# A mixed sequence model on one core: the gate behind the last scores, written out step by step

## The reference, cut to what matters

```python
x = x + _L1_attn_ref(_layernorm(x), Wqa, Wqb, Wkva, Wkvb, Wout, bout)   # latent attention, 16 heads, causal
h = _layernorm(x)
gate_logits = einsum('bsd,de->bse', h, Wg) + bg
topk_w, topk_i = top_k(gate_logits, 2); topk_w = softmax(topk_w)
w = sum(one_hot(topk_i, 8) * topk_w[..., None], axis=-2)
g = gelu(einsum('bsd,edf->bsef', h, W1) + b1)          # 8 experts, 128 -> 512
out = einsum('bsef,efd,bse->bsd', g, W2, w) + einsum('bse,ed->bsd', w, b2)
x = x + out
```

## Time and profile before

| | |
|---|---|
| median of 3 runs | 2117.47 us (2115.41 to 2117.84) |
| profiled execution | 2117.03 us, its span in the profile 2113.9 us |
| instructions | 64856 |
| PE busy | 2001.8 us (95%) |
| DVE busy | 1531.6 us (72%) |
| ACT busy | 1692.8 us (80%) |
| POOL busy | 1454.2 us (69%) |
| mean granted TensorE clock | 0.980 of full |

### The profile page before, as it was taken

The page is one execution under the profiler, slowest core; times in us unless marked ns, Lnnn a source line. Parts: engine busy times, 40 slices in busy tenths (PEclk is TensorE's granted clock), DMA queues, the critical chain, the costliest instruction groups (busy, mean ns, idle before and its releaser), DMA issues. The chain is left out here.

```text
span 2113.9 us, 64856 instructions
## 1 busy us (share of the span) xinstructions
PE 2001.8 (95%) x21603; PEld 1401.2 (66%) x21611; DVE 1531.6 (72%) x3516; ACT 1692.8 (80%) x4279; POOL 1454.2 (69%) x1662
## 2 busy tenths in 40 slices
PE   6899999999999999999999999999999998999596
PEld 3566666666666666666667666666666665666496
DVE  7777777777777777777777777777777764788654
ACT  4688888888888888898989898989898986666355
POOL 5777777777777777777777878787877762244333
PEclk8999999999999999999999999999999999999888
DMA  4222232322232222322222322223544242000023
GB/s 112 52 60 64 48 95 58 73 47 63 65 83 64 61 50 60 84 69 63 56 55 74 81 66 56 54 59 84 120 98 104 49 108 85 2 11 14 18 57 107
DMA packets 191397, 138.95 MB, mean 66 GB/s; under 512 B 47759, under 2 KB 183637, under 8 KB 191173
## 3 DMA queue, kind: packets, MB, share of 16 engines
q1 hardware_dynamic: 189028, 133.09, 26.6%
q0 software_dynamic: 2272, 4.72, 0.7%
HBM read 28.36 MB, written 14.96 MB: 20 GB/s over the span
## 5 line engine op out<-in xcount | busy, mean ns | idle before, releaser
L977 ACT ACTIVATE pr<-bank,mx 128x64 f32<-128x64 f32 x1536 | 336.9, 348 | 0.3 <-DVE mx L1080 0.2
L1162 POOL TENSOR_TENSOR qr<-t 128x512 f32<-128x512 f32 x192 | 245.8, 1280 | 121.0 <-DVE t L1060 120.9
L1059 DVE TENSOR_TENSOR t<-bank,rot_t 128x512 f32<-128x512 f32 x384 | 263.0, 685 | 88.5 <-PE bank L814 86.2
L1150 POOL TENSOR_TENSOR qr<-qr,rn 128x512 f32<-128x512 f32 x192 | 200.8, 1046 | 173.0 <-DVE rn L1031 173.0
L1060 DVE TENSOR_TENSOR t<-bank,rot_t 128x512 f32<-128x512 f32 x384 | 261.5, 681 | 0.0
L1168 POOL TENSOR_TENSOR sqh<-sq 128x512 f32<-128x512 f32 x192 | 246.0, 1281 | 0.0
L1165 POOL TENSOR_TENSOR kr<-t 128x512 f32<-128x512 f32 x192 | 245.3, 1278 | 0.0
L939 ACT ACTIVATE sq<-bank 128x512 f32<-128x512 f32 x192 | 114.4, 596 | 158.2 <-DVE t L1060 158.1
L985 ACT ACTIVATE kBD<-bank 64x512 f32<-64x512 f32 x384 | 228.9, 596 | 3.9 <-PE bank L532 1.6
L814 PE MATMUL bank<-wqkv,xs 128*128 128x512 f32 x384 | 208.3, 625 | 9.1 <-ACT sq L939 2.3
L865 PE MATMUL bank<-kBD,qT 128*32 128x128 f32 x6144 | 207.5, 276 | 0.4 <-ACT bank L919 0.3
(11 more groups left out here) (267 smaller groups left out, 4389.2 us busy)
## 6 DMA issues: line engine op xcount, KB each, us to landing
vBD<-vS SPq DMA_DIRECT2D x1152, 64.0 KB, 2.0
vBD<-vS SPq DMA_DIRECT2D x576, 32.0 KB, 1.9
wqkv<-in_L_ffn_Wqkv_dram SPq DMA_DIRECT2D x12, 768.0 KB, 6.6
rows<-const SPq DMA_DIRECT2D x4, 2244.0 KB, 11.5
wo<-in_L_ffn_Wo_dram SPq DMA_DIRECT2D x12, 256.0 KB, 2.9
t<-rows SPq DMA_DIRECT2D x39, 66.0 KB, 1.9
vBD<-in_L_ffn_W_dram SPq DMA_DIRECT2D x1, 2048.0 KB, 8.6
vBD<-in_L_ffn_W_dram SPq DMA_DIRECT2D x8, 256.0 KB, 7.1
```

Source lines behind the costliest of these rows:

```text
L977: ins = act.activation(pr[:, slot % 2, hd, :], bank[5][:, hd * 64:(hd + 1) * 64], ACT.Exp, bias=mx[:, slot % 2, hd:hd + 1])
L1059: dve.tensor_tensor(t1[:, m], src, tab[:, 0, :].unsqueeze(1).broadcast_to([P, HH, DH]), ALU.mult)
L1150: pool.tensor_tensor(x, x, rn[:, slot, half * HH:(half + 1) * HH].unsqueeze(2).broadcast_to([P, HH, DH]), ALU.mult).then_inc(norm.sem, 1)
L1162: pool.tensor_tensor(qr[:, slot].rearrange("p (h d) -> p h d", d=DH), t1[:, 0], t2[:, 0], ALU.add).then_inc(q_add.sem, 1)
```

## The change

- `pairs()` ends at s = 8; what the loop did at s = 9, 10 and 11 is written out for each engine in an order of its own. LAST = NB - 2 = 6.
- DVE: choose_place and choose_rows of sequence 5 come before normalise_values(7); the residual add of sequence 7 is followed at once by its moments; choose_member(6) comes before the normalise of 7, choose_rows(6) before choose_bias(7). The step numbers of `d_ch` follow the new order.
- A third home for rows, `xg[2]`, in the tile `wo`, with a third set of slots, is used for sequence 7, whose normalise and twin copies so no longer wait for sent rows.
- PE: the transposes of `wA` for groups 0 to 2 (sequences 0 to 5) are issued behind choose_logits(6), ahead of the output projection of sequence 7; bias groups 0 and 1 are issued ahead of the counts of sequence 6 and of sequence 7; only group 3 of the transposes and bias groups 2 and 3 follow the last count. Banks are W_BANK and B_BANK. ACT keeps the turned weights in the same order.
- The number of instructions for each kind of work stays as it was.

```diff
-        slot_u = [late[:, 216 + 4 * k:220 + 4 * k].bitcast(U32) for k in range(2)]
+        slot_u = [late[:, o:o + 4].bitcast(U32) for o in (216, 220, 232)]
         count = late[:, 224:224 + NE]
         xg = [x[:, :, :, :].rearrange("p m h d -> p (m h d)")[:, 0:NSLOT * NT * ROWN].rearrange("p (m t c) -> p m t c", m=NSLOT, t=NT)
-              for x in (t1, t2)]
+              for x in (t1, t2)] + [wo[:, :, :].rearrange("p c k -> p (c k)")[:, 0:NSLOT * NT * ROWN].rearrange("p (m t c) -> p m t c", m=NSLOT, t=NT)]
...
-        LN_STEPS, LOGIT, ROWS, ROW_SET, ROWS_END, DIFF, MEMBER, PLACE, GATE_STEPS = 3, 1, 1, 9, 12, 14, 18, 20, 20
+        LN_STEPS, ROW_SET, ROWS_END, DIFF, MEMBER, PLACE, GATE_STEPS = 3, 8, 11, 14, 18, 20, 20
+        LAST = NB - 2
+        def logit_step(g):
+            return 1 if g < LAST else ROWS_END + 1
+        def row_step(g, n):
+            return n + 1 if g + 1 < LAST else n
         TABLE = 12
+        W_BANK, B_BANK = (4, 5, 6, 6), (7, 4, 5, 0)
...
-            for s in range(1, NB + C_LAG):
+            for s in range(1, NB + 1):
...
-            link(dve, ins, g, ROWS_END + 1)
+            link(dve, ins, g, ROWS_END + 2)
...
-            pool.wait_ge(d_ch.sem, d_ch.after(g + 1, ROW_SET))
+            pool.wait_ge(d_ch.sem, d_ch.after(g + 1, row_step(g, ROW_SET)))
...
+            last = NQ * NB - 1
+            pe.wait_ge(c_ptd.sem, c_ptd.after(2 * last + 1))
+            choose_counts(pe, LAST - 1)
+            pe.wait_ge(c_pta.sem, c_pta.after(2 * last + 1))
+            choose_turn(pe, LAST, LAST % 2)
+            values(NB - 1, 2, 0)
+            values(NB - 1, 2, 1)
+            choose_logits(pe, LAST)
+            for g in range(NGR - 1):
+                choose_back(pe, g)
+            pe.wait_ge(c_nrm.sem, c_nrm.after(NB - 1))
+            for t in range(NT):
+                mm = pe.matmul(low[:, t * P:(t + 1) * P], con[:, t * P:(t + 1) * P], wout[:, :], start=True, stop=True)
+            mm.then_inc(c_y.sem, 1)
+            choose_shift(pe, 0)
+            choose_counts(pe, LAST)
+            choose_turn(pe, NB - 1, 2)
+            choose_logits(pe, NB - 1)
+            choose_shift(pe, 1)
+            choose_counts(pe, NB - 1)
...
+            choose_place(dve, LAST - 1)
+            choose_rows(dve, LAST - 1, (LAST - 1) % 2)
+            normalise_values(NB - 1)
+            choose_bias(dve, LAST)
+            dve.wait_ge(c_y.sem, c_y.after(NB - 1))
+            x = acc[:, seq_cols(NB - 1)]
+            dve.tensor_tensor(x, bank[0][:, 0:SEQ], x, ALU.add).then_inc(c_res.sem, 1)
+            gate_moments(dve, NB - 1)
+            choose_member(dve, LAST)
+            gate_normalise(dve, NB - 1, 2, False)
+            choose_place(dve, LAST)
+            choose_rows(dve, LAST, LAST % 2)
+            choose_bias(dve, NB - 1)
+            choose_member(dve, NB - 1)
+            choose_place(dve, NB - 1)
+            choose_rows(dve, NB - 1, 2)
...
+            send_rows(pool, LAST - 1, (LAST - 1) % 2)
+            gate_rsqrt(pool, NB - 1)
+            twin_rows(pool, NB - 1, 2, False)
+            send_rows(pool, LAST, LAST % 2)
+            send_rows(pool, NB - 1, 2)
+        def choose_back(pe, g):
+            k = g * TG // NT + TG // NT
+            pe.wait_ge(d_ch.sem, d_ch.after(k, row_step(k - 1, ROWS_END)))
+            if g == NGR - 1:
+                pe.wait_ge(d_wTev.sem, d_wTev.after(g - 1))
+            for t in range(TG):
+                mm = pe.transpose(bank[W_BANK[g]][0:NE, t * P:(t + 1) * P], wA[:, g * TG + t, :], ident)
+            mm.then_inc(d_wT.sem, 1)
+        def choose_shift(pe, g):
+            pe.wait_ge(d_wTev.sem, d_wTev.after(g))
+            if g == NGR - 1:
+                pe.wait_ge(c_res.sem, c_res.after(NB - 1))
+            for t in range(TG):
+                o = (g * TG + t) * P
+                mm = pe.matmul(bank[B_BANK[g]][:, t * P:(t + 1) * P], dwT[:, o:o + P], b2e[:, :], start=True, stop=True)
+            mm.then_inc(d_b2.sem, 1)
         def gate_pe(pe):
-            pe.wait_ge(d_ch.sem, d_ch.after(NB, ROWS_END))
+            pe.wait_ge(d_ch.sem, d_ch.after(NB, row_step(NB - 1, ROWS_END)))
             pe.matmul(bank[3][:, 0:NE * NT], cst("ones"), run, start=True, stop=True).then_inc(d_count.sem, 1)
-            for g in range(NGR):
-                for t in range(TG):
-                    mm = pe.transpose(bank[4 + g][0:NE, t * P:(t + 1) * P], wA[:, g * TG + t, :], ident)
-                mm.then_inc(d_wT.sem, 1)
-            for g in range(NGR):
-                pe.wait_ge(d_wTev.sem, d_wTev.after(g))
-                if g == 3:
-                    pe.wait_ge(d_tab.sem, 1)
-                for t in range(TG):
-                    o = (g * TG + t) * P
-                    mm = pe.matmul(bank[g][:, t * P:(t + 1) * P], dwT[:, o:o + P], b2e[:, :], start=True, stop=True)
-                mm.then_inc(d_b2.sem, 1)
+            choose_back(pe, NGR - 1)
+            for g in range(2, NGR):
+                choose_shift(pe, g)
+        def keep_back(act, g):
+            act.wait_ge(d_wT.sem, d_wT.after(g))
+            act.activation(dwT[:, g * GW:(g + 1) * GW], bank[W_BANK[g]][0:NE, :], ACT.Copy).then_inc(d_wTev.sem, 1)
+        def keep_gate(act, g):
+            act.wait_ge(g_back.sem, g_back.after(g))
+            act.wait_ge(d_lmm.sem, d_lmm.after(g - 1))
+            act.activation(xnG, bank[2][:, 0:SEQ], ACT.Copy).then_inc(g_out.sem, 1)
+        def gate_exp(act, g):
+            act.wait_ge(d_ch.sem, d_ch.after(g, DIFF))
+            act.activation(dexp[:, :], ddiff[:, :], ACT.Exp).then_inc(d_e.sem, 1)
         def gate_act(act):
-            for g in range(NGR):
-                act.wait_ge(d_wT.sem, d_wT.after(g))
-                act.activation(dwT[:, g * GW:(g + 1) * GW], bank[4 + g][0:NE, :], ACT.Copy).then_inc(d_wTev.sem, 1)
+            keep_gate(act, LAST)
+            for g in range(NGR - 1):
+                keep_back(act, g)
+            gate_exp(act, LAST)
+            keep_gate(act, NB - 1)
+            gate_exp(act, NB - 1)
+            keep_back(act, NGR - 1)
...
-                dve.tensor_tensor(a, a, bank[g][:, :], ALU.add).then_inc(d_tab.sem, 1)
+                dve.tensor_tensor(a, a, bank[B_BANK[g]][:, :], ALU.add).then_inc(d_tab.sem, 1)
```

More of the change, by code:

```diff
@@ L1368, in choose_bias @@
             link(dve, dve.tensor_tensor(dlg[:, :, :], bank[3][:, 0:NT * NE].rearrange("p (t e) -> p t e", t=NT),
[L1369 removed]
+                                        bgb[:, :].unsqueeze(1).broadcast_to([P, NT, NE]), ALU.add), g, logit_step(g))
         def choose_member(dve, g):
@@ L1397, in choose_rows @@
+            link(dve, dve.tensor_copy(slot_u[p], slot.rearrange("p m t -> p (m t)")), k, row_step(g, 3))
             dve.wait_ge(d_e.sem, d_e.after(g))
-            link(dve, dve.tensor_scalar(dden[:, :], dexp[:, :], 1.0, None, ALU.add), k, ROWS + 4)
-            link(dve, dve.reciprocal(dpx[:, 0, :], dden[:, :]), k, ROWS + 5)
-            link(dve, dve.tensor_tensor(dpx[:, 1, :], dexp[:, :], dpx[:, 0, :], ALU.mult), k, ROWS + 6)
-            link(dve, dve.tensor_tensor(dwx, oh, dpx.unsqueeze(3).broadcast_to([P, NSLOT, NT, NE]), ALU.mult), k, ROWS + 7)
@@ L1402, in choose_rows @@
-            link(dve, dve.tensor_copy(xg[p][:, :, :, D + 2], dpx), k, ROW_SET)
-            link(dve, dve.tensor_tensor(wA[:, ds(g * NT, NT), :], dwx[:, 0], dwx[:, 1], ALU.add), k, ROW_SET + 1)
-            link(dve, dve.tensor_tensor(run, run, member, ALU.add), k, ROW_SET + 2)
+            link(dve, dve.tensor_scalar(dden[:, :], dexp[:, :], 1.0, None, ALU.add), k, row_step(g, 4))
+            link(dve, dve.reciprocal(dpx[:, 0, :], dden[:, :]), k, row_step(g, 5))
+            link(dve, dve.tensor_tensor(dpx[:, 1, :], dexp[:, :], dpx[:, 0, :], ALU.mult), k, row_step(g, 6))
@@ L1405, in choose_rows @@
+            link(dve, dve.tensor_tensor(dwx, oh, dpx.unsqueeze(3).broadcast_to([P, NSLOT, NT, NE]), ALU.mult), k, row_step(g, 7))
+            link(dve, dve.tensor_copy(xg[p][:, :, :, D + 2], dpx), k, row_step(g, ROW_SET))
+            link(dve, dve.tensor_tensor(wA[:, ds(g * NT, NT), :], dwx[:, 0], dwx[:, 1], ALU.add), k, row_step(g, ROW_SET + 1))
+            link(dve, dve.tensor_tensor(run, run, member, ALU.add), k, row_step(g, ROW_SET + 2))
             link(dve, dve.tensor_tensor(run.rearrange("p (e t) -> p e t", e=NE), run.rearrange("p (e t) -> p e t", e=NE),
-                                        member.rearrange("p (e t) -> p e t", e=NE)[:, :, ::-1], ALU.add), k, ROWS_END)
+                                        member.rearrange("p (e t) -> p e t", e=NE)[:, :, ::-1], ALU.add), k, row_step(g, ROWS_END))
@@ L1447, in turns @@
                     if g is not None and (m, r) == (1, 1):
-                        pe.wait_ge(d_ch.sem, d_ch.after(g, LOGIT))
+                        pe.wait_ge(d_ch.sem, d_ch.after(g, logit_step(g)))
                     ev, n = (c_pta, c_ptd)[r % 2], 2 * (NQ * a + m) + r // 2
@@ L1651, in lat_dve @@
```

(2 more changed lines are left out.)

9 lines of the change are left out of this document (3 added, 6 removed).

## The result

The changed kernel takes 2106.22 us (median of 6 runs, 2105.81 to 2107.44) against 2116.93 us of the kernel before in the same set of runs: the ratio is 0.9951, with a 95% interval of 0.9939 to 0.9964. The forecast was 2107.9 us with a range of 2105.0 to 2110.5. The profiled execution took 2105.81 us, and its page gives the span and the busy times as follows. The busy times are within 0.7 us of those before (PE's weight loads, PEld, within 1.4 us), the instructions of each engine within 8, and the span is 9.9 us shorter.

A forecast was written before the change was run, and what follows sets the result against it. The gate's tail, with PE nearly idle, delays the experts, after which PE is busy throughout. Gains of 5.7 + 1.65 + 2.25 = 9.6 us take the profiled 2117.03 to 2107.4, median 2107.9 us, range 2105.0 to 2110.5.

The forecast's parts named there:

- three terms: Gains in the gate's tail: 5.7 us at sequence 7's normalise, 1.65 us from sequence 6's steps, 2.25 us at the experts' start.
- step 6: Start of the experts: rows, not bias adds, set the first up projection, at 2010.1 instead of 2019.71; 2.25 us more.
- Step 1 and 2: DVE and POOL: early choose_rows(5) and scatters, plus the third home, start sequence 7's normalise at 1989.4 instead of 1995.12; 5.7 us.
- Step 3: DVE: sequence 6's steps fill the wait for sequence 7's logits; choose_rows(7) at 1996.7 instead of 2004.06; 1.65 us of this.
- Step 4: POOL's scatters: those of sequence 6 leave before those of 7, due at 1999.1; first fetch at 2006.7, nothing lost.
- second rival: Scatters of sequences 6 and 7 stretched under DVE's dense steps, costing 2.2 us, so 2110.1 us; chance 0.09.
- Step 5: PE: twelve weight transposes and two bias groups move into earlier gaps at no cost; bias groups have 0.6 to 0.7 us cover.
- first rival: PE's clock kept full into the experts by the filled gaps, giving back 2.4 us, so 2105.5 us; chance 0.09.
- one for one: Experts: PE is busy throughout, so each microsecond they start earlier ends the kernel a microsecond earlier.
- The rival in which it stays low: Experts: the clock stays at half after PE's 4.5 us wait; held to the end, about 2155 us; chance 0.03.
- The rival in which the POOL wait stays: Scatters of sequence 5 stay late, sequence 7's rsqrt behind them; 5.7 us lost, 3.9 remain, so 2113.6 us; chance 0.04.

The follow-up runs named there:

- e2: Changed kernel with choose_rows(5) back behind the residual add of sequence 7 and the third transpose group behind the projection; 2112.39 us, ratio 0.9977 to the kernel before.
- e1: Changed kernel without the third home for rows, so sequence 7 uses home 1 again and waits for sent rows; 2106.73 us, ratio 0.9952 to the kernel before.
- e4: Changed kernel with choose_rows(6) behind the bias step of sequence 7 instead of ahead of it; 2108.78 us, ratio 0.9964 to the kernel before.
- x1: Changed kernel with DVE's steps of the last two sequences in another order; 2107.49 us, ratio 0.9953 to the kernel before.
- b0: The kernel before, unchanged, profiled once more; median 2116.47 us.
- e3: Changed kernel with all sixteen weight transposes and four bias groups back behind the last count, on the old banks; median 2108.65 us.
- e5: Same kernel as e3, run again on one chip with the changed kernel; median 2110.51 us against 2108.14 us.
- a0: The changed kernel itself, unaltered, run and profiled again; median 2108.14 us.
- x2: Changed kernel with SP's loads of the first two row numbers ahead of its wait for the scatters; 2107.09 us, ratio 0.9952 to the kernel before.
- x3: Changed kernel with the edits of x1 and x2 together; 2105.24 us, ratio 0.9942 to the kernel before.
- x5: Same kernel as x3, run again on one chip with the changed kernel; 2105.24 us against 2108.14 us.

## Why the prediction was right

The forecast was right in sign and range, and its mechanism holds in the first two of its three terms. The third term, the 2.25 us of step 6, was there in the profile that the prediction read, but it is no fixed property of the kernel before, so its share in the match is partly luck.

- Step 1 and 2, the normalise: forecast 1989.4, measured 1989.50; gain 5.7 forecast, 5.62 measured. e2 gives it back (5.3), e1 does not. Of the two means that step 2 named, the early scatters carry it; dropping the wait for sent rows was worth 0.1 to 0.3 us.
- Step 3: choose_rows(7) forecast at 1996.7, measured 1996.20. The term was 1.65 us and came out as 2.2 (7.86 in all, less 5.62). The way from the last member step to the first row step took 1.62 us instead of the 1.82 copied from the earlier trace rows: there 0.16 us were DVE's own queue at the end of a loop, which the written-out order no longer has. e4 takes 1.86 us of the term away.
- Step 4: scatter of 7 forecast at 1999.1, fetch at 2006.7; measured 1998.70 and 2006.26, with no scatter stretched. All twelve of the tail took 0.95 to 1.06 us, as in the earlier trace rows. So no run here shows what the Trainium skill says in "SBUF — State Buffer", section "SBUF: two separate sides", of GpSimd held back by VectorE; whether any of these DVE steps takes the shared port pair was not tested. The second rival falls. x1 shows the pause at its least, and still no growth.
- Step 5: the transposes ended 0.9 us ahead of the projection, bias group 0 at 1987.37 against counts at 1989.06, group 1 at 1994.33 against 1994.63: the cover there was 0.3 us, not 0.7.
- Step 6: the up projection forecast at 2010.1, measured 2009.66. The term of 2.25 us, by which the weights had held up the experts in the kernel before, was measured at 2.2 (10.05 less 7.86). It was right for the profile that it was read from and is no property of that kernel: in b0 nothing is left of it (34.68 less 26.93 is 7.75, against the 7.86 of the steps before). Nor is it shown that moving the weights brings it: in e3 and e5, with the weights behind, the up projection came as soon as with them moved. Between the first profiles the distance from the logits to the end of the span shrank by 9.9 us, between the second (b0 and a0) by 7.3. On the chip of a0, where the kernel before has a median of 2115.24 us, the change brought 7.1 us; in the first set of runs 10.7. The first rival had the right kind of cause, the clock, but looked for it in the changed kernel.
- The clock in the experts rose 5.6 us after the dense work began in the first profile of the changed kernel, near the 5.9 taken; over all profiles it was 2.4 to 5.9 us. So "one for one", by which the prediction carries an earlier start of the experts to the end of the kernel, is not exact: e4 starts them 1.84 us later and ends 0.1 us later. The two first profiles, 94.2 and 94.3 us from there to the end, happen to be alike. The rival in which it stays low, the one on the other side, found nothing for it. The rival in which the POOL wait stays describes e2, not the change.

The span shrank by 9.9 us, the profiled execution by 11.2; the other 1.3 us lie outside the span (3.13 us before, 1.81 after), of which the prediction said nothing. They vary from run to run of one kernel (1.8 to 3.7 us in the later runs of the kernel before), and no edit of the diff is behind them that a trace shows.

## What to carry to other kernels

Before a stage is overlapped or given more buffers, read which queue its inputs stand in: here an rsqrt of 1 us stood behind 4.85 us of scatters that were themselves released too late, and reordering eleven small steps was worth more than the extra buffer. Where a wait is filled, compute the distance in the new order to what then ends last (rows instead of bias adds), because the gain stops there. And where half a stage runs at half clock, profile the kernel before more than once and lay the traces on each other at a fixed instruction: a term of 2.25 us came and went with the clock, not with the code.

## What the runs showed of the hardware

- The granted clock can rise inside the bias matmuls, which use only 8 rows, and does so in some executions only: 7.13 us in one profile of the kernel before, 4.08 in the other. In the first, PE was busy for all 10 us from 2007 to 2017 and the granted clock stayed at 0.50; in b0 it rose near 2013.7, with PE busy since 2009.1. It fell near 1988 in the changed kernel with PE busy for 1.37 of 2 us before it, and in a0, the same kernel, only near 1994, 7.7 us behind the logits and not 5.3.
- A scatter starts 0.78 us after the step that releases it (L1411 ends 1997.92, scatter 1998.70 in the changed kernel; L1439 ends 2000.33, scatter 2001.11 in x1). The timeline names a later step as releaser, L1414, which ends 0.15 us ahead of it; in x1 the last step ends 0.36 us ahead, and the 0.78 to the slots stayed.
- SP's first fetch comes 1.45 us after the last scatter has landed, with the load of the row number in between (an estimate: the scatter started at 2010.27, its landing is taken 2.34 us later at 2012.6, and the fetch is at 2014.05 in the kernel before). With two row numbers loaded behind the table it comes 2.0 us after the table (2005.45 to 2007.45 in x2), in x3 and x5 as well.
